# A chain of four attention blocks: 64-row score and maximum tiles in opposite halves of TensorE, value products over two key chunks at a time

## What is computed

```python
# 0: cross attention, 20 heads of 8, 512 keys       (residual)
# 1: self attention, 20 heads of 8, 256 keys        (LayerNorm, residual)
# 2: cross attention, 20 heads of 8, 512 keys       (LayerNorm, residual), then a gated GELU layer
# 3, 4: 8 heads of 20: 256 queries over 508 context rows; the last 4 rows' queries over x
# 5, 6, feed-forward: as 1, 2, feed-forward
scores = jnp.einsum('bhqd,bhkd->bhqk', q, k) / jnp.sqrt(head_dim)
probs = jax.nn.softmax(scores, axis=-1)
out = jnp.einsum('bhqk,bhkd->bhqd', probs, v)
```

## Time and profile before

| | |
|---|---|
| median of 3 runs | 1082.56 us |
| runs | 1079.00 to 1089.43 us |
| profiled execution, its time | 1083.78 us |
| its span in the trace | 1082.0 us |
| mean granted TensorE clock | 0.981 |
| busy: TensorE matmul / VectorE / ScalarE | 96% / 64% / 62% |

### The profile page before, as it was taken

How to read it: one execution, slowest core, us unless ns; L and a number is a source line. 1 busy time by engine, 2 the same in 40 slices (tenths; PEclk the granted TensorE clock), 3 DMA queues, 4 the chain that set the end, 5 groups by cost and what they waited for, 6 DMA issues and landing times.

```text
span 1082.0 us, 21250 instructions
## 1 busy us (share of the span) xinstructions
PE 1034.7 (96%) x7808; PEld 719.5 (67%) x7808; DVE 689.4 (64%) x1603; ACT 675.4 (62%) x1400; POOL 74.0 (7%) x129
## 2 busy tenths in 40 slices
PE   8999989999998999999998998999999899999978
PEld 5656666667685666767685666676768566765646
DVE  3777757875546567875755775787555556777631
ACT  4556666766664666766765665776665556766641
POOL 3000000000002100001010000000100110000000
PEclk9899999999999999999999999999999999999995
DMA  8110001110232101010113010101021400111000
GB/s 195 42 39 17 21 22 44 30 31 11 49 77 56 25 21 45 21 31 22 35 31 89 21 26 20 45 21 31 10 60 30 103 20 22 34 25 40 11 7 7
DMA packets 31150, 40.26 MB, mean 37 GB/s; under 512 B 10324, under 2 KB 22232, under 8 KB 30728
## 3 DMA queue, kind: packets, MB, share of 16 engines
q1 hardware_dynamic: 31048, 38.89, 14.9%
HBM read 10.97 MB, written 0.66 MB: 11 GB/s over the span
## 4 chain that ended last, share of the span: by engine, by line
PE 87%; DVE 5%; ACT 4%; issue 3%; DMA 0%; POOLq 0%; POOL 0%; DVEq 0%; ACTq 0%
PE st_ps L775 18%; PE pv_ps L831 17%; PE mx_ps L794 17%; PE sp_ps L757 8%; PE sp_ps L758 7%; PE sp_ps L876 4%; PE sp_ps L858 3%; DVE mx L1221 2%; PE sp_ps L808 2%; PE sp_ps L950 2%; PE sp_ps L938 2%; PE sp_ps L989 2%; ACT probs L1062 2%; ACT oT L1069 1%; PE sp_ps L893 1%
## 5 line engine op out<-in xcount | busy, mean ns | idle before, releaser
L1221 DVE TENSOR_REDUCE mx<-mx_ps 128x1 f32<-128x512 f32 (+2 forms) x720 | 475.4, 685 | 184.4 <-PE mx_ps L794 181.1
L1062 ACT ACTIVATE probs<-st_ps 128x512 f32<-128x512 f32 x720 | 400.6, 597 | 184.3 <-PE st_ps L775 178.4
L794 PE MATMUL mx_ps<-ring,qT 128*128 128x512 f32 (+2 forms) x864 | 294.9, 400 | 6.9 <-issue 3.8
L775 PE MATMUL st_ps<-qT,ring 128*128 128x256 f32 (+1 forms) x1408 | 276.1, 298 | 5.4 <-ACT probs L1062 3.2
L775 PEld LDWEIGHTS st_ps<-qT,ring 128*128 128x128 f32 (+1 forms) x1408 | 217.8, 190 | 80.4 <-ACT probs L1062 40.6
L831 PE MATMUL pv_ps<-probs,v 128*9 128x256 f32 (+3 forms) x2944 | 223.8, 377 | 3.0 <-ACT probs L1062 2.3
L794 PEld LDWEIGHTS mx_ps<-ring,qT 128*128 128x128 f32 x864 | 143.5, 190 | 88.9 <-DVE mx L1221 45.7
L831 PEld LDWEIGHTS pv_ps<-probs,v 128*9 128x9 f32 (+2 forms) x2944 | 44.9, 90 | 64.3 <-issue 19.2
L1111 ACT ACTIVATE kdense<-sp_ps 128x512 f32<-128x512 f32 (+2 forms) x116 | 57.4, 539 | 24.4 <-PE sp_ps L876 23.9
L1049 ACT ACTIVATE ks<-sp_ps 128x320 fp32r<-128x320 f32 x80 | 35.2, 440 | 42.3 <-PE sp_ps L858 27.5
L876 PE MATMUL sp_ps<-identr,ks 128*128 128x128 f32 (+1 forms) x416 | 59.7, 279 | 0.7 <-DVE qs L1187 0.6
(11 more groups left out here) (134 smaller groups left out, 1050.2 us busy)
## 6 DMA issues: line engine op xcount, KB each, us to landing
ring<-kdense SPq DMA_DIRECT2D x256, 64.0 KB, 2.0
wb<-in_w_blk SPq DMA_DIRECT2D x4, 1400.0 KB, 9.1
ring<-kdense SPq DMA_DIRECT2D x160, 32.0 KB, 1.8
ring<-kdense SPq DMA_DIRECT2D x32, 127.0 KB, 2.3
wd<-in_w_down SPq DMA_DIRECT2D x4, 400.0 KB, 9.5
ring<-oT SPq DMA_DIRECT2D x16, 64.0 KB, 3.2
ctx_n<-in_ctx SPq DMA_DIRECT2D x4, 192.0 KB, 6.6
x<-in_x SPq DMA_DIRECT2D x4, 160.0 KB, 3.3
```

Source lines behind the costliest of these rows:

```text
L775: mm = pe.matmul(st_ps[s % N_ST][0:kr, i * a["nq"]:(i + 1) * a["nq"]], key_op(n, h)[:, c * P:c * P + kr], query_op(u, b)[:, h // of(u), :] ...
L794: mm = pe.matmul(mx_ps[o % N_MX][0:rows, j * a["nk"]:(j + 1) * a["nk"]], query_op(u, b)[:, h // of(u), tt * P:tt * P + rows], key_op(n, h) ...
L1062: nc.scalar.activation(probs[0:kr, s % N_P, 0:w], st_ps[s % N_ST][0:kr, 0:w], ACT.Exp, scale=float(a["dh"]) ** -0.5).then_inc(S["probs_rea ...
L1221: nc.vector.tensor_reduce(mx[b][0:rows, t, heads[0]:heads[-1] + 1], mx_ps[(o - 1) % N_MX][0:rows, 0:a["hpm"] * a["nk"]].rearrange("p (h k) ...
```

## The change

Scores and maxima contract over 64 rows in place of 128. A ring place has two planes of 512 keys where it had four: in partitions 0 to 63 lie the first two heads of a quad, in 64 to 127 the other two, and in each half a head has one plane, with the other head's 32 rows zero. The four DMAs per quad stay. The wide heads (attentions 3 and 4) fill a half by themselves, so they are read from `kdense` (and a new tile `kca`), without `kdma`, ring or clears. A score slot holds two heads of the same half, and slots alternate between the halves; so do maximum items, which begin with the second half. Attention 4 has two heads in a slot where it had four, which makes 736 slots out of 720. `pv` takes a run of two chunks (16 instructions for a quad's two chunks) where it took one, and `N_P` is 10. The planner has new costs, two lanes for the halves, and 95 ns for every change between rows, columns and the full array.

```diff
     3: dict(kind="enc", H=8, dh=20, sr=64, nq=SQ, nk=NENC, hps=2, hpm=1),
-    4: dict(kind="ca", H=8, dh=20, sr=64, nq=C, nk=SQ, hps=4, hpm=2),
+    4: dict(kind="ca", H=8, dh=20, sr=64, nq=C, nk=SQ, hps=2, hpm=2),
...
 N_MX = 2
-N_P = 6
+N_P = 10
 RING = 4
+RUN = 2
...
     return min(P, nk - P * c)
+def of(u):
+    return P // ATT[u]["sr"]
+def half(u, h):
+    return h % of(u) // (of(u) // 2)
+def same_half(u, qd):
+    hs = range(4 * qd, 4 * qd + 4)
+    return [[h for h in hs if half(u, h) == k] for k in range(2)]
+def runs(u):
+    n_c = -(-ATT[u]["nk"] // P)
+    return [list(range(c, min(c + RUN, n_c))) for c in range(0, n_c, RUN)]
+def items_of(u, qd):
+    a, tiles = ATT[u], q_tiles(u)
+    per = [[(t, rows, hs[i:i + a["hpm"]]) for i in range(0, 2, a["hpm"]) for t, rows in tiles] for hs in same_half(u, qd)]
+    return [item for both in zip(per[1], per[0]) for item in both]
...
                         for c in range(n_c):
-                            for h in range(4 * qd, 4 * qd + 4, a["hps"]):
-                                slots.append(dict(n=n, u=u, b=b, c=c, heads=list(range(h, h + a["hps"])),
-                                                  last=c == n_c - 1 and h + a["hps"] == 4 * qd + 4))
+                            for k, heads in enumerate(same_half(u, qd)):
+                                slots.append(dict(n=n, u=u, b=b, c=c, heads=heads, last=c == n_c - 1 and k == 1))
...
                                           slots=list(range(start, len(slots))),
-                                          items=[(t, rows, list(range(h, h + a["hpm"])))
-                                                 for h in range(4 * qd, 4 * qd + 4, a["hpm"]) for t, rows in q_tiles(u)]))
+                                          items=items_of(u, qd)))
...
         m = len(q["items"])
-        put(lo - K_LEAD, 0, ("kdma", n))
+        if ATT[q["u"]]["sr"] == 32:
+            put(lo - K_LEAD, 0, ("kdma", n))
...
         put(hi + MTR_DUE, 3, ("mtr", n))
-        for c in range(q["n_c"]):
-            last = max(s for s in q["slots"] if slots[s]["c"] == c)
-            put(last + PV_LAG, 2, ("pv", n, c))
+        for i, cs in enumerate(runs(q["u"])):
+            last = max(s for s in q["slots"] if slots[s]["c"] == cs[-1])
+            put(last + PV_LAG, 2, ("pv", n, i))
...
-    if kind == "clear":
-        return 0, [("pool", 2400)]
...
         rows = a["hpm"] * nk
-        return 4 + 0.417 * rows, [("dve", 60 + 1.05 * rows)]
+        return 4 + 0.45 * rows, [("dve", 60 + 1.05 * rows)]
...
     if kind == "st":
-        return 218, act(512)
+        return 236, act(a["hps"] * a["nq"])
     if kind == "pv":
-        return 4 * nq * 0.47, []
+        return len(runs(u)[step[2]]) * nq * 1.57, []
...
+    def lane(step):
+        if step[0] == "st":
+            return half(slots[step[1]]["u"], slots[step[1]]["heads"][0])
+        if step[0] == "max":
+            return half(quads[step[1]]["u"], quads[step[1]]["items"][step[2]][2][0])
+        return None
+    def shape(step):
+        return "rows" if step[0] in ("st", "max") else "columns" if step[0] == "pv" else "full"
+    def pe_free(step):
+        if shape(step) != mode:
+            return max(lanes) + MODE
+        return max(clock["pe"], max(lanes) if mode != "rows" else lanes[lane(step)])
...
         if pe:
-            t = clock["pe"] = max(start, clock["pe"]) + pe
+            begin = max(start, pe_free(step))
+            mode, t = shape(step), begin + pe
+            if mode == "rows":
+                lanes[lane(step)], clock["pe"] = t, begin + (pe / 2 if step[0] == "st" else 0)
+            else:
+                lanes, clock["pe"] = [t, t], t
...
         caT8 = two("caT8", [C, 32])
-        kdense = two("kdense", [P, 5, SK])
+        kdense = two("kdense", [P, 5, SK], FR)
+        kca = two("kca", [P, 2, SQ], FR)
...
         ks8 = sb("ks8", [P, 2, 8, 64], FR)
-        ring = sb("ring", [P, RING, 4, SK], FR)
+        ring = sb("ring", [P, RING, 2, SK], FR)
...
         s_warm = sem("zeros_ready")
-        def of(u):
-            return P // ATT[u]["sr"]
-        def region(u, h):
-            return h % 4 if of(u) == 4 else 2 * (h % 2) + h % 4 // 2
+        places = ring_places(quads)
+        def side(u, h):
+            k = half(u, h)
+            return slice(64 * k, 64 * k + 64)
         def key_op(n, h):
-            return ring[:, n % RING, region(quads[n]["u"], h), :]
-        ring_dmas = {n: 4 * (n // RING + 1) for n in range(len(quads))}
+            u, b = quads[n]["u"], quads[n]["b"]
+            g = h // of(u)
+            if n in places:
+                return ring[side(u, h), places[n][0], h % 2, :]
+            if u == 4:
...
+                return (kca[b][:, g, :] if g < 2 else kdense[b][:, 4, (g - 2) * SQ:(g - 1) * SQ])[side(u, h), :]
+            return kdense[b][side(u, h), g, :]
+        def query_rows(u, b, h):
+            return query_op(u, b)[side(u, h), h // of(u), :]
...
                         taken(sp, [s for s in order if s[0] == "k_tr" and s[1] == u and s[2] == b][-1])
-                        if n >= RING:
-                            sp.wait_ge(S["scores_full"], quads[n - RING]["slots"][-1] + 1)
-                        if dirty(quads, n):
-                            sp.wait_ge(S["cleared"], value["cleared", ("clear", n)])
-                        for h in range(4 * qd, 4 * qd + 4):
-                            j, g = h % of(u), h // of(u)
-                            rows = slice(a["sr"] * j, a["sr"] * (j + 1))
-                            sp.dma_start(ring[rows, n % RING, region(u, h), 0:a["nk"]].bitcast(F32),
-                                         dense_keys(u, b, g)[rows, 0:a["nk"]]).then_inc(ring_in[n % RING], 16)
+                        at, _, before = places[n]
+                        if before is not None:
+                            sp.wait_ge(S["scores_full"], quads[before]["slots"][-1] + 1)
+                        for j in range(4):
+                            rows = slice(32 * j, 32 * j + 32)
+                            sp.dma_start(ring[rows, at, j % 2, 0:a["nk"]].bitcast(F32),
+                                         kdense[b][rows, qd, 0:a["nk"]].bitcast(F32)).then_inc(ring_in[at], 16)
...
                             taken(pe, last)
-                            pe.wait_ge(ring_in[n % RING], 16 * ring_dmas[n])
+                            if n in places:
+                                pe.wait_ge(ring_in[places[n][0]], 64 * (places[n][1] + 1))
...
+                            else:
+                                taken(pe, [s for s in order if s[0] == "k_tr" and s[1] == u and s[2] == b][-1])
...
                             mm = pe.matmul(mx_ps[o % N_MX][0:rows, j * a["nk"]:(j + 1) * a["nk"]],
-                                           query_op(u, b)[:, h // of(u), tt * P:tt * P + rows],
-                                           key_op(n, h)[:, 0:a["nk"]], start=True, stop=True)
+                                           query_rows(u, b, h)[:, tt * P:tt * P + rows], key_op(n, h)[:, 0:a["nk"]],
+                                           start=True, stop=True)
...
                     elif kind == "pv":
-                        _, n, c = step
+                        _, n, k = step
...
                         a = ATT[u]
-                        mine = [s for s in quads[n]["slots"] if slots[s]["c"] == c]
-                        if c == 0 and n:
+                        n_c = -(-a["nk"] // P)
+                        mine = [s for s in quads[n]["slots"] if slots[s]["c"] in runs(u)[k]]
+                        if k == 0 and n:
...
                         pe.wait_ge(S["probs_ready"], slot_value("probs_ready", mine[-1]))
-                        if c == 0 and qd == 0:
+                        if k == 0 and qd == 0:
...
                             pe.wait_ge(S["k_high"], value["k_high", last])
-                        kr = chunk_rows(a["nk"], c)
                         for s in mine:
+                            c = slots[s]["c"]
+                            kr = chunk_rows(a["nk"], c)
...
                                                probs[0:kr, s % N_P, i * a["nq"]:(i + 1) * a["nq"]],
-                                               start=(c == 0), stop=(c == -(-a["nk"] // P) - 1), tile_position=(0, 32 * j))
-                            if s == mine[-1] and c == -(-a["nk"] // P) - 1:
+                                               start=(c == 0), stop=(c == n_c - 1), tile_position=(0, 32 * j))
...
                         if u == 4:
-                            dst = (oT[b][:, 2:4, :] if gg == 0 else kdense[b][:, 4, :].rearrange("p (g k) -> p g k", g=2))
+                            dst = (kca[b][:, :, :] if gg == 0 else kdense[b][:, 4, :].rearrange("p (g k) -> p g k", g=2))
...
                         dve.wait_ge(S["max_full"], o)
-                        nc.vector.tensor_reduce(mx[b][0:rows, t, heads[0]:heads[-1] + 1],
```

(5 more changed lines are left out.)

54 lines of the change are left out of this document (26 added, 28 removed).

## The result

The changed kernel takes **1136.86 us** (median of 4 runs, 1136.52 to 1137.09) where the kernel before takes 1081.9 (4 runs on the same chip, 1079.0 to 1089.43): a ratio of 1.050, interval 1.044 to 1.055. It is slower by 5%; the forecast had it faster by 8%.

A forecast was written before the change was run, and what follows sets the result against it. TensorE's queue was taken to set the time (busy 1034.7 of 1082.0 us). From 1083.8, less 112 (-117 + 5), plus 20 and 10 given back, came 1002, with 1 us off for the median: 1000 us, range 955 to 1065.

The forecast's parts named there:

- step 1: Scores and maxima on 64 rows: the halves run side by side, 342 us becoming 225, a saving of 117 us.
- The clock: TensorE's granted clock: no fall expected, since the change adds no wait as long as 3.78 us; no price, no chance.
- step 2: Value products over two chunks: 184 exits and entries of the column tiles fewer, 36 us saved, extra waiting costed at nothing.
- step 3: Array shape changes: 771 where there were 722, at 0.098 us each; together with two-chunk value products, net +5 us.
- step 4: Ring copies and GpSimd clears for the wide attentions go away: taken as 0, at most 4 us gained.
- step 5: Waits on other engines: 20 us come back in six VectorE-heavy stages, 10 us more from TensorE's waits for banks.
- No overlap, and the borders cost: Rival: halves do not overlap and 684 shape borders cost 0.098 us each; 1088 to 1103 us, chance 0.08.
- nothing is given back: Rival: other engines take back none of TensorE's saving; 950 to 975 us, chance 0.15 (with anything less).
- loads take turns: Rival: weight loads of the two halves cannot overlap, leaving 33 us saved; 1050 us (1038 to 1062), chance 0.20.

The follow-up runs named there:

- e4: TensorE matmul streams alone, without attention, free or paced by VectorE reductions; 512-column tiles alternating halves took 0.23 us a pair, 256-column ones 0.124.
- e2: Changed kernel in its order, but score and maximum matmuls contract over all 128 rows, without tiling; 1094.3 us, 1.009 of the kernel before.
- e5: Changed kernel in its order, with all 64-row score and maximum tiles in the first half, so nothing overlaps; 1351.8 us, 1.247 of the kernel before.
- J: TensorE stream without attention: two 128-row, 512-column matmuls to each VectorE reduction; stayed at 2.4 GHz with TensorE busy for 88% of the time.
- K: TensorE stream without attention: two 64-row matmuls in one half to each VectorE reduction; the clock fell after 5 us.
- e3: Changed kernel with value products over one chunk in place of two, halves kept; 1115.0 us, 1.028 of the kernel before.
- e10: Kernel before with two-chunk value products, ring kept at 4, 7 probability buffers and a new planner's cost; 1115.9 us, 1.030 of the kernel before.
- e6: Changed kernel with one-chunk value products and 128-row score and maximum matmuls; 1089.6 us, 1.006 of the kernel before.

## Why the prediction was wrong

- **Overlap of the halves (step 1): right.** Pairs start together, 0.23 us per pair of 512 columns, and loads overlap (e4). Whether the stream of the whole kernel lost all of the 117 us was not measured. At an equal clock a gain shows: about 5% in the stages of full clock (e2 above), and by another way, the changed kernel is at 1136.9 with 0.875 and e2 at 1094.3 with 0.975. At 9 to 11 us per 0.01 the changed kernel would be at 1027 to 1047 with e2's clock, 47 to 67 us below e2. That is an estimate from the slopes above.
- **The clock: the step that failed.** "A fall of the clock is no case of mine ... the change adds no wait of such a length that I can find." I took from the earlier trace rows that only a pause of some 4 us brings the clock down. The trace of before says otherwise in a place that I passed over:

```profile
18.00:24.00 6.00, 5.41 (x31) 4.17 (x32) 0.94 (x3) 5.41 (x14) 0.00 (x0) 0.98 0.89 211
24.00:34.00 10.00, 10.00 (x33) 8.32 (x31) 2.39 (x6) 4.83 (x14) 0.00 (x0) 0.50 0.51 118
```

The clock falls at 23.8 with no pause over 0.55 us in the 8 us ahead, and stays down for 10 us of unbroken matmuls; only 3.4 of the 41 us at the lower level belong to the earlier trace rows. Nor did it hold that no long wait was added (the pause of 7.17 us). Two things were missed. A tile of 64 rows holds the clock less well than one of 128 (e2 and e5; J and K), and the shorter stream leaves more short pauses in stages that ScalarE and VectorE pace (TensorE is idle for 103 us, and for 76 in e2). How much of the fall belongs to each was not separated; e2 and e3, idle alike, speak for the rows. Together they put 284 us instead of 41 at the lower level. For 0.106 of clock that is 95 to 117 us; from 1136.9 it leaves 1020 to 1042, the time the changed kernel would have at the clock of before. That is an estimate by these slopes, well beyond the 0.04 over which they were read.
- **Value products by two chunks (step 2): wrong sign.** The forecast had -36 us and took the wait for four exponentials at nothing. e10 costs 33, e2 against e6 some 5. Twenty changes of shape fewer gave 0.4 to 1.5 us of 2 in the cross stage above, and other stages took that back.
- **More shapes (step 3): mis-sized a little.** By start-to-start intervals in the changed kernel, a border after 256-column scores costs 0.10, as the earlier trace rows said for the value columns. After a 128-column transpose it costs 0.15 (0.204 us until the next shape starts, of which 0.053 are its columns), and 161 borders into rows come behind a matmul of 128 columns. That is 8 us above the +5.
- **Copies and clears (step 4)**: no sign of a gain or a cost in stages of full clock, and not tested by itself. The longer pause at 594.9, behind the weights in SyncE's queue, may belong here.
- **What the others give back (step 5): right in kind, short in size.** 1020 to 1042 at the old clock against 1000 leaves 20 to 42 us, and the 36 that step 2 did not give and the 8 of step 3 are enough for it; this is a sum of estimates, and no run shows it. VectorE in the stage 198 to 237.5 is at 82% (32.21 of 39.50), under the 88% that I let it reach.
- **The rivals.** "No overlap, and the borders cost" had the right sign by the wrong mechanism; "nothing is given back" and "loads take turns" are out. The true case was the one I excluded in a sentence, so it got neither a chance nor a place in the range. The lines that should have raised it were in view: stages with VectorE at 79% of the time were to lose 6 to 10 us of TensorE's work each, and TensorE was to fall below 93% busy. The Trainium skill (TensorE: Matmul & The Clock Gate, "A second HAM failure mode: psum-queue depth-cycling") describes short idle times between groups of matmuls, with banks of results in a cycle, as enough for the clock to go up and down. The trace after agrees in part: the clock falls sixteen times, eleven of them without a pause of 1 us in the 8 us ahead; but in e2, with the same banks and the same order, it falls five times, so the rows matter too. It would have been worth a rival with its own price.

## What to carry to other kernels

Before TensorE's work is cut in a kernel that other engines pace, ask what keeps its clock up: count stages in which its busy share will fall, and price the lower level at about 0.4 us per us (0.39 to 0.46 here). Look at every stretch in which the clock is down before the change, not only at the one with the longest pause. Tiles of half the rows overlap in full, and keep the clock in an unbroken stream (e4); in stages that other engines pace they trade matmul time for clock. And a saving on the busiest engine's queue is not a saving of the stage: compare the same stage, cut at the same instructions, under two orders.
